# Group 0's softmax in one form, four engine lists in another order, filler products, and two gaps around XTH

## The reference

```python
x = x + L0_xattn(layernorm(x), ctx)   # 16 heads of 16, softmax over 77 context keys
x = x + L0_ffn(layernorm(x))          # expert 0 alone: 256 -> 1024 relu -> 256, layernorm
x = x + L1_xattn(layernorm(x), ctx)   # one head of 256, softmax over 77 keys
x = x + L1_ffn(layernorm(x))          # 8 matrices of 256x256, one chosen by each position
```

## Time and profile before

| what | value |
|---|---|
| median of the runs | 272.77 us |
| profiled execution, its own time | 274.57 us |
| its span, first to last instruction | 272.7 us |
| PE busy | 251.4 us, 92% of the span |
| DVE busy | 218.5 us, 80% |
| POOL busy | 190.0 us, 70% |
| ACT busy | 160.8 us, 59% |
| mean granted clock of TensorE | 0.975 |

### The profile page before, as it was taken

How to read it: one execution, slowest core, us unless ns; L and a number is a source line. 1 busy time by engine, 2 the same in 40 slices (tenths; PEclk the granted TensorE clock), 3 DMA queues, 4 the chain that set the end, 5 groups by cost and what they waited for, 6 DMA issues and landing times.

```text
span 272.7 us, 6211 instructions
## 1 busy us (share of the span) xinstructions
PE 251.4 (92%) x2048; PEld 223.1 (82%) x2048; DVE 218.5 (80%) x573; ACT 160.8 (59%) x510; POOL 190.0 (70%) x361
## 2 busy tenths in 40 slices
PE   1977799899799999999999999999999999979991
PEld 1776577599798979999799799998889999868880
DVE  2789998999999789973999986898588676869551
ACT  2549795885263766697385887466655533354530
POOL 3347689897859797966398688888789565605474
PEclk9995999999999999999999999999999999979997
DMA  6993020010101165000001421121080000000033
GB/s 173 325 305 113 0 78 2 2 38 21 60 0 42 41 174 174 5 20 2 0 2 49 90 68 37 53 79 40 2 267 6 0 0 2 0 2 2 0 154 154
DMA packets 11156, 17.61 MB, mean 65 GB/s; under 512 B 1377, under 2 KB 7509, under 8 KB 11125
## 3 DMA queue, kind: packets, MB, share of 16 engines
q1 hardware_dynamic: 9333, 11.98, 14.5%
...
## 4 chain that ended last, share of the span: by engine, by line
PE 71%; DVE 13%; POOL 5%; ACT 4%; issue 3%; DMA 1%; SPq 0%; POOLq 0%; DVEq 0%
PE PB L273 33%; PE PB L266 13%; PE PB L470 7%; PE PB L346 5%; PE S L394 5%; PE PB L406 4%; PE S L384 4%; ACT E L1065 2%; DVE SX L664 2%; POOL E L1259 1%; DMA WKV<-in_w_k 1%; DVE SX L678 1%; POOL SM L1216 1%; DVE XTL L643 1%; POOL out_x L1312 1%
## 5 line engine op out<-in xcount | busy, mean ns | idle before, releaser
L1259 POOL TENSOR_TENSOR E<-E,SX 128x308 f32<-128x308 f32 x64 | 43.9, 713 | 10.6 <-DVE SX L681 10.4
L1065 ACT ACTIVATE E<-S,SX 128x77 f32<-128x77 f32 x128 | 39.5, 337 | 10.6 <-DVE SX L664 10.6
L273 PE MATMUL PB<-XTH,W1H 128*128 128x256 f32 x128 | 37.8, 295 | 1.5 <-DVE XTL L643 1.4
L273 PE MATMUL PB<-W2H,HH 128*128 128x256 f32 x128 | 37.4, 292 | 0.0
L273 PE MATMUL PB<-XTL,W1H 128*128 128x256 f32 x128 | 36.2, 282 | 0.0
L273 PE MATMUL PB<-XTH,W1L 128*128 128x256 f32 x128 | 36.1, 282 | 0.0
L273 PE MATMUL PB<-W2H,HL 128*128 128x256 f32 x128 | 35.6, 278 | 0.0
L273 PE MATMUL PB<-W2L,HH 128*128 128x256 f32 x128 | 35.6, 278 | 0.0
L1216 POOL TENSOR_TENSOR SM<-SM,nhalf 128x2 f32<-128x2 f32 x40 | 28.3, 709 | 3.1
L1088 ACT ACTIVATE HH<-PB 128x512 fp32r<-128x512 f32 x32 | 19.1, 599 | 17.5 <-PE PB L273 17.5
L1075 ACT ACTIVATE EW<-S 124x640 f32<-124x640 f32 x32 | 21.9, 711 | 10.9 <-PE S L394 10.8
...
## 6 DMA issues: line engine op xcount, KB each, us to landing
...
```

The costliest lines, as they stand in the source:

```text
L273: t = e.matmul(dst, a, b, start=first and j == 0, stop=last and j == n - 1)
L1065: t = e.activation(Ei[:, h * NK:(h + 1) * NK], P[:, at:at + NK], ACT.Exp, bias=SX[:, i, 0, k:k + 1], accum_out=SX[:, i, 1, k:k + 1])
L1259: t = e.tensor_tensor(Eh, Eh, SX[:, i, 2, 8 * a + h:8 * a + h + 4].unsqueeze(2).to_broadcast([128, 4, NK]), ALU.mult)
```

## The change

For group 0, `apart` is now false, so both halves of its heads go through the 8 exponentials on ACT, and DVE neither subtracts nor sums. Four lists are in another order (SP's is unchanged); the same pieces stand in them, apart from `warm`, which multiplies the identity by itself n times into a bank that nobody reads, 23 times in all in four places. Two unused tensors of 192 and 320 bytes stand before and behind XTH and XTL. The lists are cut here after what the prediction speaks of.

```diff
 def apart(g, i, a):
-    return a == 1
+    return a == 1 and g >= 1
...
         XTE = sb("XTE", [128, 2, 1024])
+        sb("apart0", [128, 48])
         XTH = sb("XTH", [128, 4, 2, 256], F32R)
         XTL = sb("XTL", [128, 4, 2, 256], F32R)
+        sb("apart1", [128, 80])
...
+            def warm(n, p):
+
+                w.wait_ge(s["m_id"], 1)
+                P = hold(("warm",), ("B", p))
+                for j in range(n):
+                    e.matmul(P[:, 0:128], ident[:, :], ident[:, :], start=True, stop=True)
...
-            keys(1); tA(0, 3); vmat(2); q(0, 1); vrep(0, 0); tA(1, 3); sc(0, 0, 0, 0); sc(0, 0, 1, 1); r_scores(2)
-            sc(0, 1, 0, 1); sc(0, 1, 1, 0); q(1, 1); tA(2, 3); tE(0, 0, 0, 0); tE(0, 0, 1, 1); tE(0, 1, 0, 0)
...
+            warm(9, 3); keys(1); tA(0, 2); q(0, 1); vmat(0); sc(0, 0, 0, 1); tA(1, 2); sc(0, 0, 1, 0); r_scores(1)
+            warm(3, 3); vrep(0, 0); warm(4, 3); sc(0, 1, 0, 1); warm(7, 3); sc(0, 1, 1, 0); q(1, 2); vrep(1, 3)
+            tE(0, 0, 0, 1); tE(0, 0, 1, 0); tA(2, 0); tE(0, 1, 0, 1); sc(1, 0, 0, 0); sc(1, 0, 1, 1); f_turn(2); q(2, 0)
...
-            setup(); mask(); stats("A", 0); apply("A", 0); wq_lo(); kf(); stats("A", 1); lo("A", 0); kbl(0)
-            apply("A", 1); vs(); stats("A", 2); ql(0); r_sign(); pivot(1); apply("A", 2); pivot(2); smax(0, 0, 0)
-            smax(0, 0, 1); f_stats(); lo("A", 1); ssum(0, 0, 0); smax(0, 1, 0); smax(0, 1, 1); ssum(0, 0, 1); vb(0)
-            ssum(0, 1, 0); r_ranks(); ql(1); r_expert(); ssum(0, 1, 1); smax(1, 0, 0); lo("A", 2); smax(1, 0, 1)
...
+            setup(); mask(); stats("A", 0); apply("A", 0); wq_lo(); kf(); lo("A", 0); stats("A", 1); kbl(0); r_sign()
+            apply("A", 1); ql(0); vs(); smax(0, 0, 0); pivot(1); smax(0, 0, 1); stats("A", 2); ssum(0, 0, 0); f_stats()
+            smax(0, 1, 0); lo("A", 1); f_norm(); ssum(0, 0, 1); smax(0, 1, 1); vb(0); apply("A", 2); pivot(2)
+            ssum(0, 1, 0); r_ranks(); ssum(0, 1, 1); ql(1); r_expert(); smax(1, 0, 0); lo("A", 2); smax(1, 0, 1); vb(1)
+            ssum(1, 0, 0); stats("A", 3); smax(1, 1, 0); ql(2); ssum(1, 0, 1); apply("A", 3); smax(1, 1, 1); x1(0)
+            ssum(1, 1, 0); stats("B", 0); r_position(); smax(2, 0, 0); ssum(1, 1, 1); apply("B", 0); f_kv(0)
+            smax(2, 0, 1); ssum(2, 0, 0); f_kv(1); lo("B", 0); smax(2, 1, 0); r_index(); kbl(1); ssum(2, 0, 1); hl(0, 0)
+            x1(1); smax(2, 1, 1); stats("B", 1); hl(0, 1); hl(0, 2); apply("B", 1); hl(0, 3); f_m(); lo("A", 3)
+            r_pairs(); lo("B", 1); ql(3); y(0); ssum(2, 1, 0); ssum(2, 1, 1); smax(3, 0, 0); smax(3, 0, 1); hl(1, 0)
...
-            rep(); w_hi(0); apply("A", 0); hi("A", 0); kba(0); apply("A", 1); qh(0); w_hi(1); hi("A", 1); apply("A", 2)
-            ex(0, 0, 0); w_hi(2); ex(0, 0, 1); ex(0, 1, 0); ex(0, 1, 1); qh(1); hi("A", 2); et(0, 0, 0); et(0, 0, 1)
...
+            w_hi(0); apply("A", 0); hi("A", 0); kba(0); qh(0); rep(); apply("A", 1); hi("A", 1); ex(0, 0, 0)
+            ex(0, 0, 1); ex(0, 1, 0); ex(0, 1, 1); apply("A", 2); qh(1); et(0, 0, 0); et(0, 0, 1); hi("A", 2)
+            et(0, 1, 0); w_hi(1); ex(1, 0, 0); qh(2); et(0, 1, 1); ex(1, 0, 1); o(0); ex(1, 1, 0); w_hi(2); f_ct()
+            et(1, 0, 0); w_hi(3); et(1, 0, 1); apply("A", 3); ex(1, 1, 1); apply("B", 0); et(1, 1, 0); ex(2, 0, 0)
+            hi("B", 0); et(1, 1, 1); w_hi(4); ex(2, 0, 1); o(1); hh(0, 0); ex(2, 1, 0); hh(0, 1); hh(0, 2); hh(0, 3)
...
-            setup(); rs("A", 0); rs("A", 1); bo(0); rs("A", 2); r_iota(); w_lo(1); bo(1); en(0, 0, 0); en(0, 0, 1)
...
+            setup(); rs("A", 0); rs("A", 1); r_iota(); en(0, 0, 0); f_rs(); rs("A", 2); bo(0); bo(1); en(0, 0, 1)
+            en(0, 1, 0); f_gb(); en(0, 1, 1); w_lo(1); en(1, 0, 0); rs("A", 3); en(1, 0, 1); en(1, 1, 0); rs("B", 0)
+            w_lo(2); en(1, 1, 1); w_lo(3); en(2, 0, 0); bo(2); w_lo(4); be(0); rs("B", 1); b2(0); en(2, 0, 1); gx(4)
+            gx(6); gx(5); en(2, 1, 0); b2(1); en(2, 1, 1); rs("Y", 0); en(3, 0, 0); one(2); rs("A", 4); be(1); gx(7)
...
```

More of the change, by code:

```diff
@@ L533, in tensor @@
[L533 to L547, removed]
@@ new lines, in vector @@
+            f_o(); ql(4); apply("B", 2); x2(1); lo("A", 5); stats("C", 1); lo("B", 2); smax(4, 0, 0); x1(3)
+            stats("B", 3); apply("C", 0); smax(4, 0, 1); hl(2, 0); ql(5); apply("B", 3); hl(2, 1); smax(4, 1, 0)
+            smax(4, 1, 1); ssum(4, 0, 0); hl(2, 2); lo("B", 3); hl(2, 3); ssum(4, 0, 1); smax(5, 0, 0); ssum(4, 1, 0)
+            ssum(4, 1, 1); apply("C", 1); starts(); y(2); cm(0); smax(5, 0, 1); hl(3, 0); ssum(5, 0, 0); stats("Y", 2)
+            hl(3, 1); x2(2); smax(5, 1, 0); x1(4); stats("C", 2); apply("A", 6); hl(3, 2); stats("B", 4); hl(3, 3)
@@ new lines, in vector @@
+            cm(1); ssum(5, 0, 1); apply("C", 2); lo("A", 6); apply("B", 4); smax(5, 1, 1); ssum(5, 1, 0); y(3)
+            apply("A", 7); ql(6); ssum(5, 1, 1); stats("Y", 3); x3_(0); x3_(1); lo("A", 7); cm(2); x2(3); smax(6, 0, 0)
+            stats("C", 3); lo("B", 4); smax(6, 0, 1); x1(5); apply("C", 3); smax(6, 1, 0); ssum(6, 0, 0); ssum(6, 0, 1)
+            ql(7); smax(6, 1, 1); hl(4, 0); cm(3); hl(4, 1); stats("B", 5); ssum(6, 1, 0); hl(4, 2); x3_(2)
+            ssum(6, 1, 1); apply("B", 5); hl(4, 3); x3_(3); smax(7, 0, 0); smax(7, 0, 1); lo("B", 5); y(4)
@@ L993, in scalar @@
+            stats("D", 4); stats("Y", 6); hl(7, 0); apply("D", 3); hl(7, 1); x2(6); hl(7, 2); hl(7, 3); stats("C", 6)
+            x3_(5); stats("D", 5); apply("C", 6); apply("D", 4); y(7); stats("Y", 7); x2(7); stats("C", 7); cm(6); pa(1)
+            apply("C", 7); pa(2); apply("D", 5); pa(3); cm(7); x3_(6); stats("D", 6); pa(4); apply("D", 6); x3_(7)
+            stats("D", 7); apply("D", 7); pa(5); pa(6); pa(7); pa(8); pa(9); pa(10); pa(11); pa(12); pa(13); pa(14)
         def scalar(e):
@@ new lines, in scalar @@
+            ex(3, 0, 0); hh(1, 1); et(2, 1, 0); ex(3, 0, 1); hh(1, 2); hh(1, 3); et(2, 1, 1); starts(); apply("A", 4)
+            o(2); ex(3, 1, 0); hi("A", 4); apply("A", 5); ex(3, 1, 1); et(3, 0, 0); et(3, 0, 1); qh(4); et(3, 1, 0)
+            et(3, 1, 1); hi("A", 5); apply("C", 0); apply("B", 2); o(3); hi("B", 2); ex(4, 0, 0); hh(2, 0)
+            apply("B", 3); qh(5); hh(2, 1); ex(4, 0, 1); hh(2, 2); xtc(0); hh(2, 3); hi("B", 3); ex(4, 1, 0)
+            apply("A", 6); ex(4, 1, 1); et(4, 0, 0); ex(5, 0, 0); et(4, 0, 1); et(4, 1, 0); et(4, 1, 1); hh(3, 0)
@@ L1330, in sync @@
+            rs("D", 2); bd(1); bd(2); b2(7); rs("D", 3); be(7); rs("Y", 6); rs("D", 4); bd(3); rs("C", 6); rs("D", 5)
+            rs("Y", 7); bd(4); rs("C", 7); rs("D", 6); rs("D", 7); bd(5); bd(6); bd(7); put(0); put(1); put(2); put(3)
+            put(4); put(5); put(6); put(7)
         def sync(e):
```

130 lines of the change are left out of this document (55 added, 75 removed).

## The result

The changed kernel took 281.93 us (median of 4 runs, 278.53 to 283.94) where the kernel before, on the same chip, took 274.04. The ratio is 1.0212 with an interval of 1.0126 to 1.0297, in the second set 1.0262, 1.0221 to 1.0304. The forecast was 269.2 us, so it was wrong in sign: the change costs 5.8 to 7.1 us.

The account below looks back on a forecast made before the run. DVE, beside it ACT, was taken to pace the start, and PE the stage behind `lo("B", 1)`. Start -2.7, gaps -1.4 and stalls +0.5 sum to -3.6 us: 272.77 becomes 269.2 us, range 266.0 to 273.6.

Parts of the forecast that it names:

- What bounds the kernel: Whole kernel: DVE, beside it ACT, paces the start; PE paces from `lo("B", 1)` at 73.24 us on.
- New stalls: POOL issues `gx(5)` ahead of `en(2, 1, 0)`, so PE's `tE(2, 1, ·)` comes late: +0.5 us, bounds 0 and 2.6.
- one microsecond as the sign that it is wrong: PE waiting more than a microsecond in all between 75 and 220 us would show the prediction wrong.
- The start: Up to `lo("B", 1)`: 1.1 us gained before `ql(1)`, 1.6 behind it; -2.7 us, bounds nothing and 4.5.
- a clock that stays up gives nothing there: From 20 to 30 us DVE sets the pace, so a higher PE clock from the fillers gains 0.
- The gaps: Moving XTH's address brings `w1` and `q` to the pace of `w2`: -1.4 us, from 2.2 to 0.6, zero a bound.
- the rival that the address is nothing: In the PE-bound stage, `w1` and `q` keep their pace despite the gaps: 270.6 us, chance 0.17.
- The fillers: 23 identity products on PE in the start take 2.5 us, up to 5 at half clock; effect 0, cost 0.5.
- The head start is given back: Rival: PE, once early, outruns POOL and DVE and waits, `en` and `hl` late: 271.3 us, chance 0.15.
- Group 0 is no sooner: Rival: ACT's four sets end after 28.15 us and `lo("B", 1)` stays at 73.2: 271.4 us, chance 0.11.
- The slower rival: ACT stands at `w_hi(4)` for W2's late second load, delaying PE's first feed-forward: 7 us gives 276.2, chance 0.10.
- Slower: Whole kernel: outcome slower by over 1%, over 275.5 us, chance 0.11.

Follow-up runs that it names:

- second set: The changed kernel run once more, unchanged, against the kernel before: 278.87 us, ratio 1.0262.
- new_old: Changed kernel without fillers, with the old lists behind `lo("B", 1)` and `ql(3)`: 271.76 us, ratio 0.9955 to the kernel before; repeats 271.45, 271.79.

## Why the prediction was wrong, point by point

**What bounds the kernel** was read rightly for the kernel before, and the short step from it was the fault: "The PE work behind that point is the same in both kernels, so the change can move the time in two ways". The work is the same, its order is not. I read the new lists closely up to `lo("B", 1)`, 73 of 273 us, and behind it priced one moved piece, as if the same work meant the same time.

**New stalls, +0.5 (0 to 2.6)**, is the step that failed. Measured: the stage from `lo("B", 1)` to `y(7)` takes 165.4 us with the new order and 157.5 with the old one behind the same start, 7.8 us more, of which 0.9 come back in the tail; in the runs the two differ by 6.2 us. The piece that I priced, `gx(5)`, does cost 2.2 us in the runs (278.01 to 275.86) and 1.4 at `y(7)`, within its bounds of 0 to 2.6, but by another way: I had it delay `en(2, 1, 0)` on POOL, while it makes six loads in a row that stop DVE and ACT. The rest are waits that I never looked for: `tB(2)` behind `rs("C", 0)`, 1.59 us, and 2.2 us in four pieces from 192 to 213 (0.74, 0.46, 0.64, 0.40). In all PE waits 4.9 us between 75 and 220, where the prediction had named one microsecond as the sign that it is wrong. Over the whole stage its idle time is 5.5 us more than with the old order; the other 2.3 us, in which PE is busy longer, stay open. The bound of 2.6 was one for one piece; the whole reorder had none.

**The start, -2.7**, measured -1.4 at `lo("B", 1)` in the one profile of the changed kernel, -0.7 on the mean of all executions, and nothing clear of the noise in the time. ACT's first set came sooner than worked out (15.66, forecast 17), yet the sets ended at 28.9, not 27.2: between the second and third I lost 3 us where the forecast had 0.5, to fillers, `vrep` and `f_stats`. So `ql(1)` stood at 30.3 (forecast 28.6, before 29.66). The part behind it, 1.6 us of DVE work counted off, held only in some executions. From `ql(1)` to `lo("B", 1)` it is 43.5 to 43.6 us with the old lists and 41.2 to 42.5 with the new ones where PE's granted clock from 36 to 38 us was 1.00; where it was 0.50 to 0.58 the new lists took 43.6 too. So "a clock that stays up gives nothing there" fails on these rows: the forecast looked at 20 to 30 us alone, and the clock behind `ql(1)` goes with about 1.5 us. In `new_old` PE runs from 52 to 238 us without a wait, so `lo("B", 1)` no longer stops it there, and an earlier one should be worth little; that is argued, not tested.

**The gaps, -1.4**: the mechanism and the pace were right, 5.46 us for 48 as for `w2` ("5.5"); the rival that the address is nothing fell. The size in the time was half, 0.7 us, not told apart from zero; in the trace 1.1, and the old order with the gaps repeats it in seven executions (157.3 to 157.6 us, without them 158.4 and 158.5). That the address modulo 512 is the reason is still not shown.

**The fillers, 0**: right in sum (0.9 us or less), wrong in price. The earlier trace rows had products of transposes, one record each; a plain product of the same shape leaves two, so 23 fillers are 46 records: 9 took 4.0 us, 3 took 0.94, 4 took 2.02 and 7 took 1.83, where the forecast had at most 5 for all.

**The rivals.** "The head start is given back" was nearest: PE does outrun the others. But it was priced at +2.1 with a chance of 0.15, as if the start's gain were the most that could be lost. "Group 0 is no sooner" came true up to `ql(1)`: ACT's four sets ended at 28.9, after 28.15, and `ql(1)` was 0.6 us later than before. The slower rival, ACT at `w_hi(4)` waiting for W2, did not come: ACT waits there 0.7 us in the changed kernel. Slower had 0.11 in all; that an order of four lists over 200 us could lose more than the start gains was no case of mine, though it needs no single mechanism: every piece moved is one more chance of a wait.
